# Cross-attention and FP4 feed-forward on one core: a setup in another order, and the weight pieces' products on GpSimd

## The reference, cut to what matters

```python
x = x + xattn(layernorm(x), ctx, ctx, Wq, bq, Wk, bk, Wv, bv, Wo, bo)
#   q = ln @ Wq.T + bq; k = ctx @ Wk.T + bk; v = ctx @ Wv.T + bv    16 heads of 32
#   scores / sqrt(32), causal mask, softmax, @ v, @ Wo.T + bo
x = x + ffn(layernorm(x), w_gate, w_up, w_down)
#   fp4_linear(x, w) = quant_dequant(x) @ quant_dequant(w).T, blocks of 16:
#     scale = max(max|x| / 6, 1e-12); round x / scale to the FP4 grid; times scale
#   h = silu(fp4_linear(x, w_gate)) * fp4_linear(x, w_up); fp4_linear(h, w_down)
```

## Time and profile before

| What | us |
|---|---|
| Three timed runs: median (lowest to highest) | 1238.52 (1235.96 to 1239.01) |
| Profiled execution: its own time | 1238.85 |
| Profiled execution: span | 1237.0 |
| PE busy in the span | 1192.6 (96%) |
| DVE busy | 1010.6 (82%) |
| ACT busy | 469.2 (38%) |
| POOL busy | 105.8 (9%) |
| First q projection on PE | 36.95 |
| First matmul of feed-forward on PE | 457.76 |

### The profile page before, as it was taken

The page is one execution under the profiler, slowest core; times in us unless marked ns, Lnnn a source line. Parts: engine busy times, 40 slices in busy tenths (PEclk is TensorE's granted clock), DMA queues, the critical chain, the costliest instruction groups (busy, mean ns, idle before and its releaser), DMA issues.

```text
span 1237.0 us, 21244 instructions
## 1 busy us (share of the span) xinstructions
PE 1192.6 (96%) x6994; PEld 1088.2 (88%) x6994; DVE 1010.6 (82%) x1771; ACT 469.2 (38%) x1141; POOL 105.8 (9%) x239
## 2 busy tenths in 40 slices
PE   6799999999999978899999999999999999999996
PEld 4688888888888868799999999999999999999994
DVE  6899999989999855887888788788788788788772
ACT  3465656565565632232232232233223223223220
POOL 2011111111111100000000000000000000000000
PEclk9999999999999999999999999999999999999998
DMA  6012111121323234225225324324333423422420
GB/s 236 20 52 77 51 61 67 51 77 52 123 90 107 97 139 151 41 56 103 56 53 101 60 53 95 65 53 92 69 54 85 76 53 73 87 53 65 87 46 25
DMA packets 91314, 94.33 MB, mean 76 GB/s; under 512 B 54396, under 2 KB 62764, under 8 KB 91155
## 3 DMA queue, kind: packets, MB, share of 16 engines
q1 hardware_dynamic: 91283, 93.95, 31.8%
HBM read 58.48 MB, written 23.94 MB: 67 GB/s over the span
## 4 chain that ended last, share of the span: by engine, by line
PE 59%; DVE 3%; issue 1%; ACT 0%; DVEq 0%; ACTq 0%
PE u_ps L171 6%; PE g_ps L171 6%; PE u_ps L172 6%; PE u_ps L173 6%; PE g_ps L173 6%; PE d_ps L1151 6%; PE g_ps L172 6%; PE d_ps L1153 6%; PE d_ps L1152 6%; PE xn_ps L285 1%; DVE hquant_amax L116 0%; DVE hquant_z L151 0%; DVE hqf L1266 0%; PE hq_ps L1124 0%; ACT hqh L1208 0%
## 5 line engine op out<-in xcount | busy, mean ns | idle before, releaser
L1252 DVE TENSOR_TENSOR hid<-u_ps,silu 128x352 f32<-128x352 f32 x128 | 66.7, 521 | 137.5 <-PE u_ps L173 136.8
L171 PE MATMUL g_ps<-wguh,xnh 128*128 128x352 f32 x512 | 169.1, 330 | 8.6 <-ACT silu L1188 3.6
L171 PE MATMUL u_ps<-wguh,xnh 128*128 128x352 f32 x512 | 168.3, 329 | 1.7 <-DVE hid L1252 1.7
L173 PE MATMUL g_ps<-wguh,xnl 128*128 128x352 f32 x512 | 166.2, 325 | 0.0
L172 PE MATMUL g_ps<-wgul,xnh 128*128 128x352 f32 x512 | 166.1, 324 | 0.0
L172 PE MATMUL u_ps<-wgul,xnh 128*128 128x352 f32 x512 | 165.6, 323 | 0.0
L173 PE MATMUL u_ps<-wguh,xnl 128*128 128x352 f32 x512 | 165.5, 323 | 0.0
L755 ACT ACTIVATE probs<-s_ps,nsmax 128x77 f32<-128x77 f32 x512 | 114.1, 374 | 119.7 <-DVE nsmax L839 119.7
L1188 ACT ACTIVATE silu<-g_ps 128x352 f32<-128x352 f32 x128 | 58.9, 460 | 221.3 <-PE g_ps L173 217.8
L1151 PE MATMUL d_ps<-wd,hqh 128*128 128x512 f32 x341 | 134.3, 394 | 0.0
L1153 PE MATMUL d_ps<-wd,hql 128*128 128x512 f32 x341 | 133.9, 393 | 0.0
(11 more groups left out here) (142 smaller groups left out, 2454.1 us busy)
## 6 DMA issues: line engine op xcount, KB each, us to landing
scale_wide<-st_dram SPq DMA_DIRECT2D x248, 88.0 KB, 4.0
xin<-in_x_dram SPq DMA_DIRECT2D x32, 256.0 KB, 2.8
x_dram<-x SPq DMA_DIRECT2D x32, 256.0 KB, 2.0
xin<-x_dram SPq DMA_DIRECT2D x32, 256.0 KB, 2.9
out_dram<-y SPq DMA_DIRECT2D x32, 256.0 KB, 2.0
wd_dram<-wd_out SPq DMA_DIRECT2D x11, 512.0 KB, 3.6
wd<-wd_dram SPq DMA_DIRECT2D x1, 5632.0 KB, 16.2
w_in<-in_L_ffn_w_gate_dram SPq DMA_DIRECT2D x11, 256.0 KB, 2.9
```

Source lines behind the costliest of these rows:

```text
L171: pe.matmul(out, lh, rh, start=(i == 0), stop=False)
L173: last = pe.matmul(out, ll, rh, start=False, stop=(i == n - 1))
L1252: dve.tensor_tensor(hid[:, c * GU_N:(c + 1) * GU_N], u_ps[:, c % 2, 0:GU_N], silu[:, c % 2, :], ALU.mult).then_inc(hid_ready, 1)
```

## The change

- **Loads.** w_nat has four buffers, so no weight load waits for PE. The order is now Wk, context, bq, bk, bv, x tile 0, Wq, piece 0, x tile 1, Wv, bo, piece 1, Wo. The setup's tensors (class `Setup`) lie where wguh is later; the columns of pieces 0 to 2 are kept free of them.
- **Order of the setup.** Wq is transposed second. Tile 0 is normalised, transposed and projected (`project_q(0)`) right behind `keys`. All of iteration 0 up to the exponentials now stands in the setup, with piece 2, and `run` begins at iteration 1. The low parts of Wo (`weight_low(3)`) and piece 2 stand last on DVE.
- **Biases.** bk and bv enter as one more matmul of one row against ones: four of 154 columns in `keys`, one of 512 in each `values`. The copies to kbd (eight) and vext (two) go from DVE to ACT. The values are formed in o_ps, and `weight_transposed(3)` waits for their copies.
- **Products.** `divide` and `rescale` of all 33 pieces go from DVE to POOL, in the loops too.

```diff
@@ setup, SP @@
-            load_weight(1, Wv)
-            for dst, row in ((bv_all, bv), (bo_all, bo)):
-                sp.dma_start(dst[:], row.rearrange("(a n) -> a n", a=1).to_broadcast(dst.shape)).then_inc(rows_loaded, 16)
+            sp.dma_start(bias_nat[:], bq.rearrange("(c p) -> c p", p=P)).then_inc(in_loaded, 16)
+            for dst, row in ((bk_row, bk), (bv_row, bv)):
+                sp.dma_start(dst[:], row.rearrange("(a n) -> a n", a=1)).then_inc(bias_loaded, 16)
+            load(0)
+            load_weight(1, Wq)
             load_piece(0)
-            load(0)
-            load_weight(2, Wq)
+            load(1)
+            load_weight(2, Wv)
+            sp.dma_start(bo_all[:], bo.rearrange("(a n) -> a n", a=1).to_broadcast(bo_all.shape)).then_inc(rows_loaded, 16)
             load_piece(1)
-            load(1)
             load_weight(3, Wo)
@@ POOL @@
+            def divide_piece(n):
+                wquant.divide(pool, n + 1, w_in[:, n % 2, :])
+
+            def rescale_piece(n):
+                if reached(n):
+                    pool.wait_ge(wT_done, n)
+                wquant.rescale(pool, n + 1, w_q[:]).then_inc(wq_ready, 1)
+
+            def iteration(a, n, down=None):
+                if piece(n):
+                    divide_piece(n)
+                    rescale_piece(n)
+                if valid(a + 2):
+                    row_scale(a + 2)
+                    add_bias(a + 2)
@@ PE, keys and values @@
                 for c in range(EC):
+                    out = kp[:, c // 2, (c % 2) * 256:(c % 2) * 256 + B * CTX]
                     for d in range(EC):
...
+                    last = pe.matmul(out, bk_row[0:1, c * P:(c + 1) * P], ones[0:1, :], start=False, stop=True)
...
-                pe.wait_ge(wth_ready, 2 * EC)
+                pe.wait_ge(wth_ready, 3 * EC)
...
+                pe.matmul(o_ps[0:CTX, b, :], ones[0:1, 0:CTX], bv_row[0:1, :], start=False, stop=True).then_inc(v_done, 1)
@@ PE, weight_transposed @@
+                    if i == 3 and n % TP < 2:
+                        pe.wait_ge(v_ready, n % TP + 1)
@@ ACT, setup @@
             weight_high(0)
             weight_high(1)
+            xn_high(0)
             wquant.shift(act, 1)
+            keys()
+            q_copy(0)
+            weight_high(2)
             piece_high(0, False)
+            values(0)
+            xn_high(1)
             wquant.shift(act, 2)
-            xn_high(0)
+            exps(0)
+            values(1)
+            weight_high(3)
             piece_high(1, False)
-            weight_high(2)
-            weight_high(3)
-            run(act, iteration)
+            wquant.shift(act, 3)
+            piece_high(2, False)
+            run(act, iteration, 1)
@@ DVE, iteration @@
                     wquant.negate(dve, n + 1)
-                    wquant.divide(dve, n + 1, w)
...
-                if piece(n):
-                    piece_quantised(n)
@@ DVE, setup @@
+            norm_stats(0)
             biases()
-            iteration(-2, 0)
-            iteration(-1, 1)
-            values(0)
-            values(1)
-            weight_low(2)
+            piece_scales(0)
+            norm_apply(0)
+            norm_stats(1)
+            weight_low(1)
+            xn_low(0)
+            piece_rounded(0)
+            norm_apply(1)
+            piece_scales(1)
+            q_bias(0)
+            piece_low(0, False)
+            xn_low(1)
+            piece_rounded(1)
+            norm_stats(2)
+            score_max(0)
+            norm_apply(2)
             weight_low(3)
-            keys()
-            run(dve, iteration)
+            piece_scales(2)
+            piece_low(1, False)
+            piece_rounded(2)
+            piece_low(2, False)
+            run(dve, iteration, 1)
```

More of the change, by code:

```diff
@@ L1 @@
 from contextlib import ExitStack
+import numpy as np
 import concourse.bass as bass
@@ L174, in split_matmuls, with __init__, row @@
     return last
+ROW = 2 * FF
+KEPT = 3 * P
+ROOM = ROW - KEPT
+class Setup:
+    def __init__(self, nc):
+        with ExitStack() as sctx:
+            def row(*tiles):
+                sctx.enter_context(nc.sbuf_tensor(f"kept_{tiles[0][0]}", [P, KEPT], F32))
+                made = [sctx.enter_context(nc.sbuf_tensor(name, shape, F32)) for name, shape in tiles]
+                used = sum(int(np.prod(shape[1:])) for _, shape in tiles)
+                sctx.enter_context(nc.sbuf_tensor(f"left_{tiles[0][0]}", [P, ROOM - used], F32))
+                return made
+            self.w_nat = [row((f"w_nat{i}", [P, EC, E]))[0] for i in range(4)]
+            self.wkt, self.wvt = row(("wkt", [P, EC, E]))[0], row(("wvt", [P, EC, E]))[0]
+            self.cin, self.ctxT = row(("cin", [CTX, B, E]), ("ctxT", [P, EC, B, CTX]))
+            self.bk_row, self.bv_row, self.bias_nat, self.ones = row(
+                ("bk_row", [1, E]), ("bv_row", [1, E]), ("bias_nat", [EC, P]), ("ones", [1, B * CTX]))
 class Shared:
@@ L181, in __init__ @@
         sb = lambda name, shape, dt=F32: ctx.enter_context(nc.sbuf_tensor(name, shape, dt))
+        self.setup = Setup(nc)
+        self.wguh, self.wgul = sb("wguh", [P, EC, 2 * FF], F32R), sb("wgul", [P, EC, 2 * FF], F32R)
         self.ident = sb("ident", [P, P])
@@ L185, in __init__ @@
         self.minus_one, self.over_qmax = sb("minus_one", [P, 1]), sb("over_qmax", [P, 1])
-        self.wguh, self.wgul = sb("wguh", [P, EC, 2 * FF], F32R), sb("wgul", [P, EC, 2 * FF], F32R)
         self.xin = sb("xin", [P, RING, E])
@@ L386, in attention, with run @@
         LOOPS = [(4, TB), (TB + 1, GU_PIECES - 2), (GU_PIECES, T - 2)]
-        def run(eng, iteration):
-            a = 0
+        def run(eng, iteration, a):
             for lo, hi in LOOPS + [(LAST + 1, LAST + 1)]:
@@ L492, in _, with row_scale @@
         def _(pool):
-            def tile(t):
+            def row_scale(t):
                 pool.wait_ge(mv_ready, t + 1)
@@ L517, in _ @@
             pool.memset(vext[:, :, :, :, HD:VW], 1.0).then_inc(const_ready, 1)
+            pool.memset(ones[:], 1.0).then_inc(const_ready, 1)
             pool.memset(kbd[:], 0.0).then_inc(zeroed, 1)
             pool.memset(vbd[:], 0.0).then_inc(zeroed, 1)
-            pool.wait_ge(const_ready, 3)
+            pool.wait_ge(const_ready, 4)
             pool.wait_ge(pool_consts, 3)
-            pool.wait_ge(rows_loaded, 16 * 2)
-            tile(0)
-            with pool.Fori(1, T) as t:
-                tile(t)
+            row_scale(0)
+            divide_piece(0)
+            row_scale(1)
+            rescale_piece(0)
+            pool.wait_ge(rows_loaded, 16)
+            add_bias(0)
+            add_bias(1)
+            divide_piece(1)
+            row_scale(2)
+            rescale_piece(1)
+            add_bias(2)
+            divide_piece(2)
+            rescale_piece(2)
+            run(pool, iteration, 1)
             for t in range(2):
@@ L694, in _ @@
             weight_transposed(1)
+            transpose_xn(0)
             keys()
+            project_q(0)
+            weight_transposed(2)
             transpose_piece(0)
+            transpose_q(0)
             values(0)
-            transpose_xn(0)
+            transpose_xn(1)
+            scores(0)
             values(1)
+            weight_transposed(3)
             transpose_piece(1)
-            weight_transposed(2)
-            weight_transposed(3)
-            run(pe, iteration)
+            transpose_piece(2)
+            run(pe, iteration, 1)
         @block.scalar
```

134 lines of the change are left out of this document (68 added, 66 removed).

## The result

| | before | changed |
|---|---|---|
| Median of 14 runs each (lowest to highest), us | 1239.45 (1235.91 to 1241.83) | 1244.74 (1242.20 to 1253.43) |
| Ratio, 95% interval | | 1.0061 (1.0042 to 1.0081) |
| Profiled execution's own time / span | 1238.85 / 1237.0 | 1242.20 / 1240.3 |
| q projection of tile 2 on PE | 59.67 | 65.50 |
| Last w_ps matmul of attention | 455.23 | 461.23 |

The kernel became slower by 0.6%. The ratio goes by the means, 1246.6 against 1238.9, which a few long executions pull up; the medians differ by 0.4%. The forecast was 1246.5, range 1238 to 1258.

What follows compares the result with a forecast made beforehand. PE sets the loop period, with DVE's cycle only 0.05 to 0.10 us behind. 1238.85 + 5.1 (setup) + 2.8 (loops) = 1246.75; with the median 0.33 lower, 1246.4, written as 1246.5; range 1238 to 1258.

Steps and rivals of the forecast that it cites:

- The setup term: Setup and first iteration: exponentials, Wo and piece 2 in series end last, tile 2's projection at 64.8, +5.1 us.
- The first q projection: Setup, PE behind keys: begins at 23.6 after transposes 1.0, keys 5.5 and a clock loss of 1.5; ends at 26.5.
- the first rest: Setup, PE ahead of Wq's fourth block: some 3 us idle, then 3 us at half clock, a loss of 1.5.
- The half clock behind the last rest: PE behind its rest for piece 2: slow clock adds 1.1 us between the projections of tiles 1 and 2.
- the bias matmuls: Setup, PE in keys and values: counted within the durations there, given no price of their own.
- The loop term: 23 loop turns: products on POOL lengthen DVE's cycle beyond its slack, 0.12 us per turn, +2.8 us.
- Its cycle: Loops: chain from smax through exponentials, product, magic and rounding to smax; +0.80 by POOL, -0.60 by w_q, net +0.20.
- the slack: Loops: room in DVE's cycle before it delays PE, inferred as 0.05 to 0.10 us per turn.
- rival 3: Loops lose nothing as the slack holds +0.20, rests do not lower the clock, setup +2.4: 1241 us; chance 0.17.
- rival 1: Loops: POOL's rescale blocks DVE's nsmax through shared ports, 0.2 per turn, 4.6 us, to 1251; chance 0.12.
- Feed-forward: Stage from 457.76 to the span's end: nothing the diff touches, 779.2 us unchanged.
- Costed at nothing: Four load buffers, twelve DMAs into vbd and POOL's row scale and addition: hidden, 0 us.

Runs made afterwards that it cites:

- experiment 2: Changed kernel with the scales of piece 2 on DVE ahead of Wo's low parts, its shift earlier on ACT: 1241.73 us, ratio to before 1.0024.
- experiment 3: Changed kernel with piece 2's transposes on PE behind tile 1's q projection and tile 0's probability transposes: 1242.08 us, ratio to before 1.0035.
- experiment 6: Changed kernel with the edits of experiment 2, experiment 3 and experiment 5 together: 1236.81 us, ratio to before 0.9982.
- experiment 11: The kernel of experiment 5 without the bias matmuls, key and value biases left out of the result: 1239.72 us, ratio to before 1.0000.
- experiment 4: Changed kernel with eight useless matmuls in PE's rest ahead of piece 2's transposes: 1241.72 us, ratio to before 1.0024.
- experiment 7: Changed kernel with one more rescale on POOL per loop turn, into an unread tile: 1265.46 us, ratio to before 1.0201.
- experiment 8: Changed kernel with one more divide-sized product on POOL per loop turn, into an unread tile: 1260.06 us, ratio to before 1.0162.
- experiment 9: Kernel before the change with only the allocation of wguh and wgul moved ahead of ident and four small tensors: 1237.09 us, ratio to before 0.9986.
- experiment 10: The kernel of experiment 6 with both products of all pieces back on DVE: 1241.97 us, ratio to before 1.0024.
- experiment 12: The kernel of experiment 6 with biases added on DVE, without bias matmuls and ACT's copies to kbd and vext: 1235.22 us, ratio to before 0.9957.
- experiment 5: Changed kernel with three useless matmuls in PE's rest ahead of the second weight's fourth block: 1243.77 us, ratio to before 1.0028.

## Why the prediction was right, and where it was not

**Direction and size** were right: +8 forecast by the two terms, +5.3 measured by the medians, +7.7 by the means. But of the two terms only one was there, and a third was missing.

**The setup term** (+5.1) was right, and in most steps: nsmax over at 39.1 (38.97), the exponentials at 42.7 (42.56), Wo at 46.5 (46.33), piece 2 at 53.1 (52.58), the projection of tile 1 at 54.0 (53.40), that of tile 2 at 64.8 (65.50). PE's rest of 8 us was 7.26, and half clock stood behind it. That the chain to piece 2 ends last was shown by shortening it and by moving piece 2 (experiments 2, 3 and 6).

Three sizes inside it were off and offset one another. The first q projection was forecast at 23.6 and came at 22.90 only because two errors met: the 1.5 us for the first rest did not come in this execution, and keys took 6.7 us (16.19 to 22.90), not 5.5. There a bias matmul takes 0.45 and not 0.27, and the 16 others take 4.9 together, against 4.1 where no bias stands between them (experiment 11). The half clock behind the last rest was put at 1.1 behind tile 1's start and cost 2.4 in all (experiment 4); this is most of why the measured term is 5.8 and not 5.1, though tile 1's projection came 0.6 early. What I put "in the sum" without a price of its own, the bias matmuls, is 3.0 to 3.6 us of the loss (experiment 11).

**The first rest** was a yes or no, not a term: I wrote 1.5 us for it. In two thirds of the executions it costs nothing. In one third it costs 7 to 8.5 us of the setup (piece 1's transposes at 51.87 in experiment 7 and 53.26 in experiment 2, instead of 44.77), since keys and the first q projection then run at half clock. These long executions lift the changed kernel's mean by 2.9 us over that of its short ones, but its median by only 0.8.

**The loop term** (+2.8) failed. Its cycle was right (experiment 8: growth of the chain less the slack), and so was the slack, 0.05 to 0.10 written and 0.13 measured in the changed kernel. The step that failed is "the nearest row for a product of two 128x512 inputs on POOL is the addition to xin, 1.29 us": the products take 1.06. With this the cycle grows by 0.60 - 0.60 = 0, nothing to be covered. With 1.29 in its place the measured rows would give 0.60 + 0.23 - 0.60 - 0.13 = 0.10 per turn, 2.3 us, close to what was written. The spacing still at 12.64 was named as the sign of rival 3, nothing in the loops. That half of it came true, though by the product's duration and not by the slack; its other half, a setup loss of 2.4, did not.

**The shared ports** (rival 1) exist, and not only in experiment 7. In the changed kernel's setup nsmax took 0.64 at 39.54, ending with POOL's w_q at 40.16; a quant_scale of 128x32 took 1.23 instead of 0.18 at 20.93, beside POOL's additions to xin; and the first nsmax of iteration 1 took 0.65 at 63.70. The two in the setup cost nothing that the chain shows: the exponentials still took 3.56, and DVE rested 5.80 behind quant_ninv. In the loops the ports cost nothing only because with 1.06 us POOL ends as nsmax begins. Experiment 7 has the longer POOL: nsmax is held by 0.83, and less the slack of 0.13 that is 0.70, against the 0.68 by which the spacing grew. A product of 1.29 would, by this estimate, have held nsmax by some 0.2. Both terms hang on the one duration.

**Feed-forward** "holds nothing that the diff touches: 779.2 us stay" failed: it is 2.7 us shorter. 2.1 of them come from the place of its tensors in SBUF (experiment 9). The other 0.6 lie at the stage's two ends, where the clock also falls, and their cause was not tested. The diff did show it: it moves the allocation.

**The total** was in part luck. Against the profiled execution the sum was 4.6 us too high: 2.8 that the loops did not lose and 2.7 that feed-forward gave back, less 0.7 in the setup and 0.2 in the rest of attention. The median came within 2 us of the forecast because it stands 2.5 above the profiled execution: 1.8 because that one is the lowest of the short ones, 0.8 through the long ones.

**Costed at nothing** and rightly so: the four buffers (PE waited 0.24 us for the load of Wq, ahead of its longer rest for wql), the twelve DMAs into vbd (the last was issued by 53.37, first use at 62.96), POOL's row scale.

## What to carry to other kernels

Work moved off an engine that is not the bound gains nothing by its busy time; ask what cycle of waits it stood in, and whether the new engine's latency, handoff included, is under what was removed plus the slack. In a setup the chain that ends last counts: a small matmul, a copy or the order of two lines on it is paid nearly in full, and a rest of PE on it may be paid twice, through the clock. Before saying that a stage is untouched, see whether a tensor that it reads has moved; and before crediting a gain of 0.2% to a new order, take off what such a move gives by itself. Where some executions are long and others not, compare like with like, since mean, median and the one profiled execution can each tell a different difference.

## What the runs showed of the hardware

- A rest of PE of about 2.6 us ahead of keys was followed by half clock in some executions and not in others of the same program (2.66 us in the changed kernel's profile: full; 2.59 and 2.65 in those of experiments 2 and 7: half). Rests of 1.86, 1.88 and 1.93 us were followed by half clock in experiments 10 and 12, rests of 1.88 and 1.77 in the kernel before were not. Once fallen ahead of keys, the clock stayed at 0.50 from 16.6 to 33.6 (experiment 2); behind the rest of 7.26 ahead of piece 2 it was back within 6 us. Three matmuls of no use in the rest ahead of keys kept it at full in the profiles of experiments 5 and 6.
- In the loops POOL takes 1.06 us for 128x512 times a scale that is broadcast over 16 elements, and 1.28 for the sum of two full 128x512 tensors. Two such products in the setup took 1.28 and 1.29 (at 13.31 and 19.61); each began beside a DVE tensor_scalar of 128x512, which ran its usual 0.54.
- A DVE tensor_scalar of 128x6 or 128x32 beside a POOL instruction ended with it: nsmax took 1.00 us instead of 0.17 and ended 0.03 behind POOL's product (experiment 7), quant_ninv took 0.81 instead of 0.18 and ended at 23.39, POOL's second addition to xin at 23.35 (the changed kernel's setup).
- The time of a feed-forward tile depended by 0.3% (23.47 against 23.39 us) on the order in which tensors are allocated in SBUF, with a pattern that repeats every three tiles in the slower one.
